# A graph convolution's second layer: its table split three chunks ahead with half of the work on ScalarE, its index lists fetched before the table is ready, the upper bound applied before the scatter, and each root product issued in two halves

## What is computed

```python
def _graph_conv_max(x, src, dst, W_rel, b, W_root):
    agg = jax.ops.segment_max(x[src], dst, num_segments=N)
    agg = jnp.where(jnp.isfinite(agg), agg, 0.0)
    return agg @ W_rel.T + b + x @ W_root.T
h = relu(_graph_conv_max(layernorm(x), src, dst, W1_rel, b1, W1_root))
h = relu(_graph_conv_max(h, src, dst, W2_rel, b2, W2_root))
x = x + h
# then 8 experts: each takes the 512 tokens of the highest softmax probability,
# gelu(selected @ W1 + b1) @ W2 + b2, weighted, added to the rows it took
```

## Time and profile before

| | |
|---|---|
| median of 3 runs | 992.68 us (989.93 to 992.88) |
| the profiled execution | 991.74 us |
| its span, first to last instruction | 989.9 us |
| busy: TensorE / VectorE / ScalarE / GpSimd | 693.8 / 674.0 / 259.1 / 565.9 us |
| mean granted TensorE clock (1 is 2.4 GHz) | 0.879 |
| layer 0 | about 127 to 421 us from the span's start |
| tile 10, table split in it | 430.3 to 495.3 us |
| experts | from about 827 us to the end |

### The profile page before, as it was taken

One profiled execution on the slowest core, in us unless ns is written; L12 is line 12 of the kernel. 1 busy time (PEld: TensorE's weight loads), 2 busy tenths in 40 slices (PEclk: granted clock), 3 DMA queues, 4 the chain that ended last, 5 costly groups with the idle time before them and its releaser, 6 DMA issues.

```text
span 989.9 us, 9615 instructions
## 1 busy us (share of the span) xinstructions
PE 693.8 (70%) x2488; PEld 313.8 (32%) x2523; DVE 674.0 (68%) x1222; ACT 259.1 (26%) x369; POOL 565.9 (57%) x551
## 2 busy tenths in 40 slices
PE   0319286875887888634588858888886414999997
PEld 0215132332333333211143424334433312444442
DVE  3679947888788878635588878888889695231210
ACT  0265151212222221111243314441332100222222
POOL 5655347777777767543156677567667004456533
PEclk9859687997999999785699979998998755999999
DMA  5716537766777766563257777677666604557646
GB/s 139 229 17 211 161 104 207 216 199 186 213 215 205 216 197 201 183 194 113 69 170 214 223 213 239 195 214 238 197 178 178 225 0 111 101 89 116 137 48 80
DMA packets 65780, 164.33 MB, mean 166 GB/s; under 512 B 16592, under 2 KB 20988, under 8 KB 65719
## 3 DMA queue, kind: packets, MB, share of 16 engines
q0 software_dynamic: 41440, 126.86, 47.5%
q1 hardware_dynamic: 17006, 17.17, 6.2%
q10 hardware_dynamic: 7288, 19.76, 6.0%
HBM read 144.44 MB, written 19.18 MB: 165 GB/s over the span
## 4 chain that ended last, share of the span: by engine, by line
PE 39%; DVE 27%; issue 14%; DMA 10%; POOL 4%; ACT 4%; DVEq 2%; POOLq 0%; ACTq 0%; SPq 0%
PE pp L1165 10%; DMA mem<-tab,ic 7%; DVE acc L899 7%; PE pp L1489 6%; PE pp L1476 6%; PE prow L1136 6%; DVE weights L910 6%; PE prow L1103 3%; POOL mem L846 3%; PE prow L1124 2%; DVE mem L1346 2%; PE pp L1487 1%; POOL mem L379 1%; PE prow L520 1%; DVE mem L445 1%
## 5 line engine op out<-in xcount | busy, mean ns | idle before, releaser
L846 POOL DMA_INDIRECT mem<-tab,ic x372 | 393.9, 1059 | 223.0 <-issue 118.1
L1165 PE MATMUL pp<-weights,slots 128*128 128x512 bf16 x1165 | 303.3, 407 | 124.6 <-DVE acc L899 65.6
L899 DVE TENSOR_TENSOR acc<-acc,pp 128x1024 f32<-128x1024 f32 x180 | 219.2, 1218 | 55.0 <-PE pp L1165 48.9
L1165 PEld LDWEIGHTS pp<-weights,slots 128*128 128x128 bf16 x1200 | 117.7, 103 | 313.7 <-issue 114.2
L910 DVE TENSOR_TENSOR weights<-weights,mem 128x1024 f32<-128x1024 f32 x129 | 158.1, 1226 | 18.8 <-DVE weights L910 11.9
L1136 PE MATMUL prow<-weights,aggT 128*128 128x512 f32 x160 | 81.3, 635 | 13.7 <-ACT aggT L1213 13.7
L1528 POOL DMA_INDIRECT out<-mem,node_of x32 | 50.3, 1572 | 69.4 <-ACT mem L1506 67.0
L1457 DVE COPY weights<-prow 128x512 f32<-128x512 f32 x32 | 20.8, 687 | 100.7 <-PE prow L1103 100.7
L1124 PE MATMUL prow<-weights,rootT 128*128 128x512 f32 x160 | 74.0, 605 | 0.0
L1489 PE MATMUL pp<-weights,mem 128*128 128x512 f32 x128 | 63.5, 618 | 0.0
L1476 PE MATMUL pp<-weights 128*128 128x512 f32 x128 | 58.2, 609 | 0.9 <-DVE weights L1457 0.9
(11 more groups left out here) (348 smaller groups left out, 761.2 us busy)
## 6 DMA issues: line engine op xcount, KB each, us to landing
slots<-ttd ACTq DMA_DIRECT2D x20, 640.0 KB, 6.2
mem<-tab,ic POOLq DMA_INDIRECT x372, 3.7
weights<-in_L_ffn_W SPq DMA_DIRECT2D x9, 512.0 KB, 10.7
weights<-in_L_ffn_W ACTq DMA_DIRECT2D x7, 512.0 KB, 4.1
xnd<-xin ACTq DMA_DIRECT2D x10, 256.0 KB, 3.2
mem<-in_x SPq DMA_DIRECT2D x2, 1120.0 KB
tab<-mem SPq DMA_DIRECT2D x1, 2240.0 KB
weights<-in_L_gnn_W_rel SPq DMA_DIRECT2D x2, 1024.0 KB, 12.1
```

The source lines that it names most:

```text
L846: g.indirect_dma_start(ring[:, h * PAIR + k, :], None, tables[l], bass.IndirectOffsetOnAxis(ic[:, j * PAIR + k:j * PAIR + k + 1], 0))\
L899: v.tensor_tensor(acc[:, :, :], acc[:, :, :], pp[j % 2][:, :, :], ALU.max).then_inc(S["pa"], 1)
L1165: ins = t.matmul(pp[j % 2][:, i, :], sel[u][:, j * KP + i, :], hot[:, j, w, :], start=w == 0, stop=w == 2)
```

## The change

1. `clamp(q)`: in layer 0 VectorE writes `min(own_row[q], TOP)` into `stage[:, q, :]`, behind picked pair 2 of the next tile (the last one behind the layer), and GpSimd's scatter waits for it (`hc`) and sends `stage` in place of `own_row`.
2. `high` goes to ScalarE as a plain copy to bf16. VectorE keeps one subtraction per chunk (`rest`) and `lowest`.
3. In tile 10, VectorE does `rest` of chunks 0 to 3 and `lowest` of 0 to 2 ahead of `first_three`; in the loop it does `rest` of chunk `j + 3` and `lowest` of chunk `j + 2` ahead of `pe_pair(k, j)`. The gathered pairs stand one step later.
4. SyncE issues layer 1's two first index loads ahead of its wait for the scatters.
5. `root_product` stands as chunks 0 and 1 behind picked pair 5 and chunks 2 and 3 behind picked pair 6.

```diff
@@ -244,7 +244,7 @@
         pl = ps("pl", [P, 512])
 
         names = """x dst small dnx gt gfree gedge gmax edge general w fw fw2 tab src dstf rec recs xs
-            ready done fin rT rTe aT aTe gn h sc xin x2 xn nT nTe lg lge xns bn rc ra fb2 b2 b2l hh hr hm hl nmx exp
+            ready done fin rT rTe aT aTe gn h sc xin x2 xn nT nTe lg lge xns bn rc ra fb2 b2 b2l hc hh hr hm hl nmx exp
             apart_s warm apart_g apart_v out add neg bits bias pairs pa merge mask
             li gr xt xte hb ge ob oe""".split()
         S = {n: sem("s_" + n) for n in names}
@@ -770,10 +770,18 @@
             rows, maxima = (m.rearrange("p (n j) -> p n j", j=4) for m in
                             (weights[:, 8 * C * D:8 * C * D + 4 * N], mem[:, 0:4 * N]))
             features = tables[l][0:N, :].rearrange("n (p j) -> p n j", p=P)
+            def load_indices(i, b):
+
+                s.dma_start(ic[:, b * SLOTS:(b + 1) * SLOTS], idx1[:, bass.ds((i * 2 + b) * SLOTS, SLOTS)])\
+                    .then_inc(s_ic[l][b], 16)
+
             if l == 0:
                 s.wait_ge(S["xs"], 16 * NQ)
                 after(s, ct, n_wraw)
             else:
+                for b in range(2):
+                    s.wait_ge(s_ic[0][b], (n_pairs_s // LAP) * 16 + 16)
+                    load_indices(0, b)
                 s.wait_ge(S["sc"], 16 * NQ)
             with s.If(good_s == 0):
                 s.dma_start(rows, features).then_inc(S["gt"], 16)
@@ -791,17 +799,11 @@
                 after(s, cv, n_meta)
                 n_pairs_s = s.value_load(meta1[0:1, NQ:NQ + 1], min_val=NQ * MINP // 2, max_val=NQ * LCAP // 2)
 
-            def load_indices(i, b):
-
-                s.dma_start(ic[:, b * SLOTS:(b + 1) * SLOTS], idx1[:, bass.ds((i * 2 + b) * SLOTS, SLOTS)])\
-                    .then_inc(s_ic[l][b], 16)
-
-            for b in range(2):
-                after(s, ca, n_idx1s[b])
-                if l:
-                    s.wait_ge(s_ic[0][b], (n_pairs_s // LAP) * 16 + 16)
-                load_indices(0, b)
-            after(s, ca, n_idx1)
+            if l == 0:
+                for b in range(2):
+                    after(s, ca, n_idx1s[b])
+                    load_indices(0, b)
+                after(s, ca, n_idx1)
             if l:
                 for i, (c0, c1) in enumerate(HPARTS):
                     for lo, hi in PARTS:
@@ -858,8 +860,8 @@
             if l == 0:
 
                 for q in range(NQ):
-                    g.wait_ge(S["h"], q + 1)
-                    g.indirect_dma_start(tab2, bass.IndirectOffsetOnAxis(nodeo[:, q:q + 1], 0), own_row[q], None)\
+                    g.wait_ge(S["hc"], q + 1)
+                    g.indirect_dma_start(tab2, bass.IndirectOffsetOnAxis(nodeo[:, q:q + 1], 0), stage[:, q, :], None)\
                         .then_inc(S["sc"], 16)
 
 
@@ -927,13 +929,15 @@
                     v.wait_ge(S["done"], first_pair + lo + SUBS)
                     v.tensor_tensor(accg, in_ring(lo + 1), in_ring(lo + 2), ALU.max).then_inc(S["done"], 3)
 
-            def high(c):
-
-                v.wait_ge(s_hx[HGROUP[c]], 32)
-                v.tensor_scalar(hot[0:CN, c, 0, :], stage[0:CN, c, :], TOP, None, ALU.min).then_inc(S["hh"], 1)
+            def clamp(q):
+
+                v.wait_ge(S["h"], q + 1)
+                v.tensor_scalar(stage[:, q, :], own_row[q], TOP, None, ALU.min).then_inc(S["hc"], 1)
+
+            def rest(c):
+
                 v.wait_ge(S["hh"], c + 1)
-                v.scalar_tensor_tensor(stage[0:CN, c, :], stage[0:CN, c, :], TOP, hot[0:CN, c, 0, :], ALU.min, ALU.subtract)\
-                    .then_inc(S["hr"], 1)
+                v.tensor_tensor(stage[0:CN, c, :], stage[0:CN, c, :], hot[0:CN, c, 0, :], ALU.subtract).then_inc(S["hr"], 1)
 
             def lowest(c):
 
@@ -1019,24 +1023,27 @@
                     pool_pair(lo + m)
                     pool_pair(lo + m + 1)
                 elif k == NQ:
-                    high(0)
-                    high(1)
+                    rest(0)
+                    rest(1)
                     lowest(0)
-                    high(2)
+                    rest(2)
                     lowest(1)
+                    rest(3)
+                    lowest(2)
                     first_three(k, lo)
-                    pe_pair(k, 1)
-                    for j in range(2, PAIRS):
-                        if j + 1 < NC:
-                            high(j + 1)
-                        lowest(j)
-                        if j == 5:
+                    for j in range(1, PAIRS):
+                        if j + 3 < NC:
+                            rest(j + 3)
+                        if j + 2 < NC:
+                            lowest(j + 2)
+                        pe_pair(k, j)
+                        if j == 6:
                             with v.Fori(3, m) as i:
                                 pool_pair(lo + i)
+                        if j == 7:
+                            pool_pair(lo + m)
                         if j == 8:
-                            pool_pair(lo + m)
-                        pe_pair(k, j)
-                    pool_pair(lo + m + 1)
+                            pool_pair(lo + m + 1)
                 else:
                     first_three(k, lo)
                     pe_pair(k, 1)
@@ -1046,6 +1053,8 @@
                         pe_pair(k, 3)
                         guess(q - 1)
                     else:
+                        if q:
+                            clamp(q - 1)
                         pe_pair(k, 3)
                     pe_pair(k, 4)
                     pe_pair(k, 5)
@@ -1077,7 +1086,9 @@
                 v.wait_ge(S["xin"], 16 * NQ)
             for q in range(NQ):
                 vec_tile(l * NQ + q)
-            if l:
+            if l == 0:
+                clamp(NQ - 1)
+            else:
 
                 cv.link(v.tensor_scalar(j15[:, :], jji[:, :], J - 1, None, ALU.bitwise_and))
                 cv.do(v.tensor_copy(jf[:, :], j15[:, :]))
@@ -1182,8 +1193,11 @@
                     root(k)
                 pairs(k, (5,))
                 if k != NQ:
-                    root_product(k, range(C))
-                pairs(k, (6, 7, 8, 9))
+                    root_product(k, (0, 1))
+                pairs(k, (6,))
+                if k != NQ:
+                    root_product(k, (2, 3))
+                pairs(k, (7, 8, 9))
                 if l and q:
                     turn_rows(q - 1)
                     logits(q - 1)
@@ -1219,9 +1233,20 @@
 
             def middles():
 
-                for c in range(NC):
+                def high(c):
+                    a.wait_ge(s_hx[HGROUP[c]], 32)
+                    a.activation(hot[0:CN, c, 0, :], stage[0:CN, c, :], ACT.Copy).then_inc(S["hh"], 1)
+
+                def middle_part(c):
                     a.wait_ge(S["hr"], c + 1)
                     a.activation(hot[0:CN, c, 1, :], stage[0:CN, c, :], ACT.Copy).then_inc(S["hm"], 1)
+
+                high(0)
+                high(1)
+                for c in range(NC):
+                    middle_part(c)
+                    if c + 2 < NC:
+                        high(c + 2)
 
             def refine(q):
```

## The result

The changed kernel takes 964.05 us in the median of four runs (963.2 to 968.59), the kernel before 992.54 beside it. The ratio is 0.9728, with a 95% interval of 0.9699 to 0.9757. A second set of runs gave 965.17 against 991.43, ratio 0.9718 (0.9693 to 0.9743). So the gain is 26.3 to 28.5 us.

What follows compares the result with a forecast made beforehand. Tile 10 was taken as bound by a chain from engine to engine, with no engine full. The terms -23.2 - 1.2 + 0.3 + 0 = -24.1 took 992.7 to 968.6 us, range 965 to 975.5.

Steps and rivals of the forecast that it cites:

- Part A: Tile 10 behind 445.12: splitting chunks ahead lets VectorE's work run in 24.3 us instead of 47.5, -23.2 us.
- the 0.9 us for the loop's register work: Tile 10's sum: three to four starts at 0.2 to 0.3 us cost back about 0.9.
- TensorE at the low clock: Tile 10: 2.72 us per picked pair would not hold VectorE up; taken as 0, +1 for the upper bound.
- The rival in which transfers bound tile 10: Third pair 2 us later and last chunks holding up `rest` by 3 us: 974.8 us; chance 0.10.
- Part B: Handover from layer 0 to tile 10: clamp +0.5, gathers 2.0 and table loads 0.8 earlier; -1.2 us, bounds 0 and -2.
- One sign: Profile after, handover: the gathers starting some 0.5 us behind the scatter's landing.
- Part C: Nine clamps inside layer 0, 0.42 us each ahead of picked pair 3's maximum, mostly covered: +0.3 us, range 0 to 0.5.
- the rival in which a clamp waits for an issue to end: Layer 0: waits of at most 0.95 us overrun the room in nine tiles, +6.2, giving 974.8 us; chance 0.05.
- The room: Layer 0, ahead of picked pair 3's maximum: 0.69 us for a clamp of 0.42 plus a semaphore.
- clamps without cover: Layer 0: all nine clamps show, 9 x 0.43 = 3.9 us, giving 972.5 us; chance 0.07.
- Part D: Root product in halves: VectorE's wait moves from pair 6 to pair 7, sum unchanged; 0 us, bounds -1.5 and +1.
- The rival on the slower side: Split root product makes VectorE wait 1.8 us for pair 7 in 18 tiles, +32.4, giving 1001 us; chance 0.04.

## Why the prediction was right, and where it was short

**Part A, the look-ahead.** Forecast 47.5 to 24.3 us, measured 47.51 to 22.78. The mechanism is shown by removal from both sides: without the look-ahead the stage goes back to 44.68, with it and the high parts on VectorE it is 25.56. The size was 1.5 us short, in three terms of the forecast's sum. The largest is the 0.9 us for the loop's register work, which cost nothing: it is 1.13 us from the maximum's start to that of the gathered pair that follows the loop's head, no more than between other neighbours. Another 0.3 us is overlap: 25 neighbours by 0.08 us are 2.0, where I had taken 1.5; the trace has the 2.0, less 0.15 us of idle ahead of the merge. The last 0.2 us are instructions a little shorter than the rows of before, 24.62 us busy instead of 24.85.

One link of the round was misread, without effect on the sum. The middle part does not stand between the subtraction and the lowest part: the one at 454.36 in the earlier trace rows is of chunk `j + 1` and begins behind the lowest part of chunk `j`, so it lies beside the round.

**TensorE at the low clock** was forecast as harmless, and was. It did pairs 3 to 5 in a row behind 447.22, at a granted clock of 0.50 until 450, and stood at the full clock (six matmuls in 1.47 us) from 454 on. The rival in which transfers bound tile 10 is out: no subtraction in the stage had idle time ahead of it, and the gathered pairs came earlier, not later. The gathers had landed in time, as forecast; GpSimd's wait for a free slot fell from 12.12 us to 4.67.

**Part B, the handover.** Forecast -1.2; merge to gathered pairs shrank by 1.0 in both traces against that of the kernel before, and by 1.5 against the halves alone. Taking the early index loads away costs 1.7 in the trace. The clamp cost 0.46 us with its semaphores (0.73 us from the output rows to the scatter instead of 0.27), as forecast. One sign was missed: the gathers were to start 0.5 us behind the scatter's landing, and started 1.5 us behind it. The chain that ended last has the scatter's landing at 425.45, register and queue steps of SyncE and GpSimd until 426.20, and 0.78 us more ahead of the first gather's issue at 426.98. The table loads gained more than forecast, 1.4 us instead of 0.8 from the end of the output rows.

**Part C, the clamps.** Forecast +0.3. The ten took 426 to 463 ns, median 428. Four of them began while GpSimd was issuing a gather, and an issue began during five others, so the rival in which a clamp waits for an issue to end (0.95 us) is out in this trace. By the rule of the Trainium skill that the forecast named ("SBUF — State Buffer", Who interferes with whom), and with that issue, a clamp would take up to 1.4 us, an estimate; here the measurement decides against it. In the ten other traces with clamps one of the hundred is longer than 0.5 us, 0.64, in the kernel with a look-ahead of two. The room was as read: one tile of the six wide ones, answering to the earlier trace rows:

```profile
192.01 0.43 DVE L935 TENSOR_SCALAR weights<-mem 128x512 f32<-128x512 f32 x1 [1.01 <-ACT mem L1232]
192.68 2.55 DVE L901 TENSOR_TENSOR acc<-acc,pp 128x1024 f32<-128x1024 f32 x2 [0.24 <-PE pp L1176]
```

1.01 + 0.43 + 0.24 is the old wait of 1.68. The stage of layer 0 is 1.7 us longer than in the trace of before, where at most 1 was forecast. But 1.4 of it stand in tile 1, which takes 28.24 us in the kernel with the halves and no clamps too. The tiles 2 to 9 take 227.69 us before and 227.97 with the halves alone, and with clamps 228.02, 228.04, 228.35 (late index loads) and 227.68 (root product whole). So nothing near the 3.9 us of clamps without cover shows; a cost of 0.3 as forecast is as small as the scatter.

**Part D, the halves.** Forecast 0, measured a ratio of 0.9999 alone, and 0.4 us slower, inside the scatter, when they were taken away. The rival on the slower side is out: the wait moved and did not grow.

**The sum.** The two stages that changed give 24.7 + 1.0 = 25.7 us, and the medians of the second set 26.3. The first set's 28.5 has an interval from 24 to 30 us, which holds 25.7. So of the 4.6 us by which 964.05 lies under the forecast of 968.6, 1.6 have a cause in parts A to C, and the other 3 are not tied to anything. The profiled execution of the first set is itself 3.6 to 5.4 us above its siblings, and the last section shows where 3 us of it went.

## What to carry to other kernels

Where no engine is full and each waits for the next, count one round's links; the gain from working ahead is the round minus the fullest engine's share of it, here 5.8 - 2.8 us a round, and 0.46 more for the part that moved to ScalarE. What had lain under the waits, here the gathered pairs, comes back as time of its own. Moving work off an engine on such a chain gives only its own length, and here splitting a block between two waits that stand back to back gave nothing. After such a change read what is left ahead of the full engine: the next gain was a wait for transfers that two rounds could fill.

## What the runs showed of the hardware

**TensorE's clock differs between executions at the same instructions.** The product behind tile 11's merge, first in the profiled execution of the first set, then in that of the second:

```profile
498.50 3.67 PE L1147 MATMUL prow<-weights,aggT 128*128 128x512 f32 x4 [0.69 <-ACT aggT L1227]
```

```profile
499.50 1.98 PE L1147 MATMUL prow<-weights,aggT 128*128 128x512 f32 x4 [0.69 <-ACT aggT L1227]
```

The 5 us of work ahead were the same to 0.01 us: the last picked pairs, idle 1.05, four transposes, idle 0.69. The granted clock of the slow one is 0.55 of 2.4 GHz from 498.4 to 502.2 us, that is, mostly the lower of the two levels, and 1.00 on both sides of it. Tile 12 took 31.27 instead of 29.15 us for it. In the second set the same happened behind tile 14's merge (3.60 us for the four) and cost 1.7 us in tile 15, and in the first behind tile 15's (2.88 us) and cost 1.9 in tile 16. These three tiles make 2.3 of the 3.2 us between 272.54 and 269.30 in the table. A trace of one execution is good to about that much.

**The same kernel takes 7 to 9% longer on some chips, and a few tiles hold most of it.** The kernel before took 991, 1064 and 1082 us on three chips. Of the changed kernel, layer 0 took 256.3 us on the first and 287.8 on the third, merge 10 to merge 19 took 269.3 and 301.2, and from the last merge on 227.0 and 231.6, while the stage that VectorE sets took 22.78 on both. Of these 63.4 us in the two layers, 41.7 stand in tiles 4, 7, 14 and 17. Tiles 5 and 8 took 26.47 us on both chips.

It isn't the gathers alone. In those four tiles ScalarE takes up the aggregate 4.9 to 17.0 us after VectorE wrote it, where the first chip has 0.8 to 1.3 us, and this lateness adds up to 31 us. The worst case is tile 14: TensorE's transposes were done at 609.35, and ScalarE, which had issued a transfer at 607.93, began here:

```profile
625.59 0.60 ACT L1227 ACTIVATE aggT<-prow 128x512 f32<-128x512 f32 x1 [17.39 <-remote]
```

TensorE stood still for 16.2 us while GpSimd went on issuing gathers. The traces of the other kernels on the second and third chip show ScalarE late in tiles 4, 14 and 17 too. The trace names no engine that released it ("remote"), so the cause stays open.
